# Layer 2 attention: a different table of steps for projections, value products and the copy of the inverses

## The reference

```python
def _L2_xattn_ref(x, context, mask, Wq, Wkv, Wout, b_out):
    HEADS = 16
    DIM_HEAD = 64
    SCALE = DIM_HEAD ** (-0.5)
    q = x @ Wq.T
    kv = context @ Wkv.T
    k, v = jnp.split(kv, 2, axis=-1)
    ...
    sim = jnp.einsum('bhid,bhjd->bhij', q, k) * SCALE
    sim = jnp.where(mask[:, None, None, :], sim, max_neg)
    attn = jax.nn.softmax(sim, axis=-1)
    out = jnp.einsum('bhij,bhjd->bhid', attn, v)
    out = out.transpose(0, 2, 1, 3).reshape(B, Nq, HEADS * DIM_HEAD)
    return out @ Wout.T + b_out
...
x = x + _L2_xattn_ref(_layernorm(x, axis=-1), ctx_1024, mask_BxS2_bf1, L2_xattn_Wq, L2_xattn_Wkv, L2_xattn_Wout, L2_xattn_b_out)
```

## Time and profile before

| | us |
|---|---|
| median of 3 executions | 1757.13 (1757.09 to 1757.54) |
| profiled execution | 1760.41 |
| its span | 1758.5 |
| mean granted clock | 0.926 |
| batch 0 from 494.56 | 51.27 |
| batch 1 from 545.83 | 61.81 |
| batch 2 from 607.64 | 65.05 |
| batch 3 from 672.69 | 63.47 |
| batch 4 from 736.16 | 61.81 |
| batch 5 from 797.97 | 61.81 |
| batch 6 from 859.78 | 61.82 |
| batch 7 from 921.60 to the end of its last inverse products, 981.80 | 60.20 |

### The profile page before, as it was taken

How to read it: one execution, slowest core, us unless ns; L and a number is a source line. 1 busy time by engine, 2 the same in 40 slices (tenths; PEclk the granted TensorE clock), 3 DMA queues, 4 the chain that set the end, 5 groups by cost and what they waited for, 6 DMA issues and landing times. The chain is left out here.

```text
span 1758.5 us, 44254 instructions
## 1 busy us (share of the span) xinstructions
PE 1535.7 (87%) x16764; PEld 804.3 (46%) x16764; DVE 1303.6 (74%) x3513; ACT 1032.9 (59%) x2227; POOL 569.5 (32%) x618
## 2 busy tenths in 40 slices
PE   5886999997669999999999899979799896999976
PEld 3532344433424444444554556655466652333333
DVE  5636778885878777677777789956899666799847
ACT  2331666665846555556555389854689631777764
POOL 0306656521010000000000289915799303342210
PEclk9895999998869999999999899999999985899997
DMA  5124333301010000000000000010100002322100
GB/s 167 34 31 134 76 80 67 66 14 49 1 38 3 8 2 9 8 3 9 28 3 3 8 1 1 0 40 9 48 1 0 1 14 74 55 43 50 30 2 24
DMA packets 60284, 54.21 MB, mean 31 GB/s; under 512 B 9610, under 2 KB 52798, under 8 KB 59974
## 3 DMA queue, kind: packets, MB, share of 16 engines
q1 hardware_dynamic: 59238, 51.32, 12.1%
q10 hardware_dynamic: 864, 0.39, 0.1%
HBM read 30.59 MB, written 1.05 MB: 18 GB/s over the span
## 5 line engine op out<-in xcount | busy, mean ns | idle before, releaser
L1926 ACT ACTIVATE probs_l2x<-probs_l2x,nmax_l2x 128x512 f32<-128x512 f32 x256 | 182.8, 715 | 193.5 <-DVE nmax_l2x L1797 193.5
L1797 DVE CUSTOM_DVE_ANT_0 probs_l2x<-s_ps_l2x,mask_b_l2x 128x512 f32<-128x512 f32 x256 | 166.6, 689 | 120.5 <-PE s_ps_l2x L2007 120.1
L1072 DVE CUSTOM_DVE_ANT_0 junk_l1x<-s_ps_l1x,mask_b_l1x 128x512 f32<-128x512 f32 x256 | 166.3, 687 | 50.3 <-PE s_ps_l1x L1273 46.0
L1075 DVE TENSOR_REDUCE nmax_l3x<-s_ps_l3x 128x1 f32<-128x512 f32 x256 | 163.7, 683 | 33.6 <-PE s_ps_l3x L1273 31.9
L1134 ACT ACTIVATE pT_l1x<-st_ps_l1x 128x1024 f32<-128x1024 f32 x128 | 131.2, 1025 | 79.9 <-PE st_ps_l1x L1258 79.5
L1809 DVE STREAM_TRANSPOSE pT_l2x<-probs_l2x 128x512 f32<-128x512 f32 x256 | 166.4, 688 | 0.0
L2007 PE MATMUL s_ps_l2x<-kT_l2x_first,q_l2x 64*32 64x512 f32 x2048 | 147.5, 634 | 11.3 <-DVE nmax_l2x L1797 10.5
L2023 PE MATMUL pv_ps_l2x<-pT_l2x,v_l2x_first 32*64 32x256 f32 x4096 | 137.7, 385 | 2.6 <-issue 2.6
L1740 POOL TENSOR_TENSOR spread_l2x<-inv_l2x,consts 128x512 f32<-128x512 f32 x16 | 17.6, 1101 | 324.5 <-DVE inv_l2x L1816 324.5
L2618 POOL TENSOR_TENSOR rn_l2a_first<-ssc_l2a_first,consts 128x16 f32<-128x16 f32 x28 | 109.1, 3897 | 20.2 <-DVE ssc_l2a_first L2645 20.0
L2788 ACT ACTIVATE probs_l2a<-minus_s_l2a,nmax_l2a 128x128 f32<-128x128 f32 (+1 forms) x256 | 106.1, 424 | 9.5 <-DVE nmax_l2a L2693 9.5
(11 more groups left out here) (531 smaller groups left out, 3574.9 us busy)
## 6 DMA issues: line engine op xcount, KB each, us to landing
mask_i_l1x<-in_mask SPq DMA_DIRECT2D x8, 512.0 KB, 4.2
maskT_i_l1x<-in_mask_t SPq DMA_DIRECT2D x8, 512.0 KB, 4.9
kT_l1x_first<-parts_l1x_first SPq DMA_DIRECT2D x60, 64.0 KB
kT_l3x_first<-parts_l3x_first SPq DMA_DIRECT2D x60, 64.0 KB
q_l1x<-parts_l1x_first SPq DMA_DIRECT2D x90, 32.0 KB
q_l3x<-parts_l3x_first SPq DMA_DIRECT2D x90, 32.0 KB
ctxT_l0x<-in_ctxT SPq DMA_DIRECT2D x9, 256.0 KB, 3.1
rows_l0x<-in_ctx SPq DMA_DIRECT2D x9, 256.0 KB, 4.2
```

The lines of the kernel that those rows point to most:

```text
L1072: dve.tensor_tensor_reduce(out=junk[w][:], in0=s_ps[w][:], in1=mask_b[b % 2][:, j, :], scale=-1.0, scalar=3e38, op0=ALU.add, op1=ALU.min, ...
L1075: dve.tensor_reduce(to, s_ps[w][:], AX.X, ALU.max, negate=True).then_inc(m.s_drained[w].sem, 1)
L1797: dve.tensor_tensor_reduce(out=probs[n % 4][:], in0=s_ps[w][:], in1=mask_b[b % 2][:], scale=-1.0, scalar=3e38, op0=ALU.add, op1=ALU.min, a ...
L1926: act.activation(probs[n % 4][:], probs[n % 4][:], ACT.Exp, bias=nmax[:, b % 2, n:n + 1], scale=-1.0, accum_out=sums[:, r, w, qb:qb + 1]). ...
```

## The change

The tables of steps are other ones. Value products stand in steps 3, 5 and 7 of a round, five, five and six blocks, where they stood in steps 1 to 7. Keys, queries and values are projected two to a step, mostly in steps without value products. V 6 and V 7 of a batch move to step 0 of the next batch (`after_batch`), the turning of the next batch's rows moves from step 7 to step 6, behind V 0 and V 1, and the output projection from steps 10 and 12 to 13 and 14, with the moments from step 13 to 14. In batch 7 the values V 2 to V 7 are projected in steps 8 to 10. On ScalarE the copy of the inverses comes behind the step's drains instead of ahead of them.

```diff
--- before.py
+++ after.py
@@ -1640,19 +1640,21 @@
 
     XT, Q, K, V, OUT, LOCAL = range(6)
     NQ, NV = NG // 2, 2 * CPB
-    this_batch = {0: [(K, 4), (K, 5), (K, 6)], 1: [(K, 7)], 2: [(Q, 2)], 3: [(Q, 3)], 4: [(V, 0)], 5: [(V, 1)], 6: [(V, 2)], 7: [(V, 3)],
-                  14: [(V, 4), (V, 5)], 15: [(V, 6), (V, 7)]}
-    next_batch = {7: [(XT, 0)], 8: [(K, 0), (K, 1), (K, 2)], 9: [(K, 3)], 11: [(Q, 0)], 13: [(Q, 1)]}
-    last_batch = {10: [(OUT, 0)], 12: [(OUT, 1)]}
-    end_values = {8: [(V, 4), (V, 5)], 9: [(V, 6), (V, 7)]}
+    this_batch = {1: [(K, 4), (K, 5)], 2: [(K, 6), (K, 7)], 4: [(Q, 2), (Q, 3)], 6: [(V, 0), (V, 1)], 8: [(V, 2), (V, 3)],
+                  14: [(V, 4)], 15: [(V, 5)]}
+    after_batch = {0: [(V, 6), (V, 7)]}
+    next_batch = {6: [(XT, 0)], 9: [(K, 0), (K, 1)], 10: [(K, 2), (K, 3)], 12: [(Q, 0), (Q, 1)]}
+    last_batch = {13: [(OUT, 0)], 14: [(OUT, 1)]}
+    end_values = {8: [(V, 2), (V, 3)], 9: [(V, 4), (V, 5)], 10: [(V, 6), (V, 7)]}
     for_local = {10: [0], 11: [1], 12: [2], 13: [3], 14: [4], 15: [5]}
-    blocks_of = {1: range(0, 3), 2: range(3, 6), 3: range(6, 8), 4: range(8, 10), 5: range(10, 12), 6: range(12, 14), 7: range(14, 16)}
+    blocks_of = {3: range(0, 5), 5: range(5, 10), 7: range(10, 16)}
 
     def step_jobs(b, s):
         end = b + 1 == B
         jobs = [(f, b - 1, n) for f, n in last_batch.get(s, ()) if b > 0]
         own = end_values if end and s >= QB else this_batch
         jobs += [(f, b, n) for f, n in own.get(s, ()) if b > 0 or f == Q]
+        jobs = [(f, b - 1, n) for f, n in after_batch.get(s, ()) if b > 1] + jobs
         jobs += [(f, b + 1, n) for f, n in next_batch.get(s, ()) if not end]
         if end:
             jobs += [(LOCAL, b, n) for n in for_local.get(s, ())]
@@ -1867,7 +1869,7 @@
                             invert_sums(n - 1)
                         for job in steps[b, s]:
                             drain(job)
-                        if s == 13 and b > 0:
+                        if s == 14 and b > 0:
                             out_moments(b - 1)
                         if s == 15 and b > 0:
                             out_scale(b - 1)
@@ -1943,10 +1945,10 @@
                         n = ROUNDS * b + s // QB
                         if ahead(b, s)[0] < B:
                             exponentials(*ahead(b, s))
+                        for job in steps[b, s]:
+                            drain(job)
                         if s % QB == 0 and n >= 2:
                             copy_inv(n - 2)
-                        for job in steps[b, s]:
-                            drain(job)
                 copy_inv(LAST - 1)
                 for job in behind[0:TPB]:
                     drain(job)
```

## The result

The changed kernel takes 1770.88 us (median of 6, 1764.98 to 1772.73) against 1757.11 (6, 1756.22 to 1757.54): ratio 1.0075, 95% interval 1.006 to 1.0091. It is slower by 13.8 us; forecast was 8. The profiled execution took 1770.07, its span 1768.2.

The account below looks back on a forecast made before the run. TensorE's own work plus its waits was taken to bound the stage. Without the clock the batches sum to +2.8 us, the clock adds +5.5, total +8.3: forecast 1765 us against 1757.13, range 1756 to 1774.

Parts of the forecast that it names:

- Part 1: TensorE's work in every batch: fewer groups of value products and paired projections save 2.64 us a batch.
- Part 2: First step of a round: the third key projection leaves, and its bank wait of 1.82 us goes, twice a batch.
- Part 3: Round's start: copy behind drains delays multiply and maxima; step 3's scores wait 2.07 us, K 6 0.39, together 2.46.
- Part 4: Step 6: turning the next batch's rows, third job behind two values, waits for a bank, +1.02 us a batch.
- The steady batch: Batches 2 to 6: each takes 61.47 us against 61.81, −0.34, together −1.7, slow clock steps apart.
- Batch 0: First batch of the stage: moved projections and low-clock steps make it 53.1 us against 51.3, +1.8.
- Batch 7: Last batch: +4.0 us; first round 28.0 against 28.9, second 34.6 against 29.7, through more values and late local tables.
- The clock: TensorE at round starts: idle stretches bring 8 half-clock steps at 1.5 us, less 6.45 before, +5.5 us.
- clock as before: Rival at round starts: same chain of waits but four slow steps as before, 1760 us; chance 0.20.
- every round: Rival at round starts: a slow step in all 14 rounds, +18.8, 1776 us; chance 0.10 for every round or nearly.
- the chain is hidden: Rival at round starts: the multiply does not hold step 2's maxima, batch 56.55 us, kernel 1726; chance 0.05.
- Half of it: Rival at round starts: drains delay the copy under 0.96 us or maxima start without the full gap, 1756; chance 0.13.

## Why the prediction was right, point by point

The forecast was 1765, slower with 0.68; measured is 1770.9, within the range. The sum had +8.3 and measured is +13.8: the clock was taken 5.2 too small and the rest of the stage 1.3, and 1.0 of that does not show in the medians. The spans of time between events came out to a few hundredths of a microsecond, the clock did not; the forecast held because its range was wide enough for that.

- **Part 1 (fewer groups, −2.64 a batch)**: right. The old and new tables with the copy in the same place differ by 2.5, waits taken off, and the profile after has value groups of 80, 80 and 96 instructions.
- **Part 2 (K 6's wait goes)**: right, in all 13 rounds.
- **Part 3 (the copy's chain)**: right in each event: copy, multiply, maxima, scores at T+4.24, 5.30, 6.60, 7.90, then K 6's wait of 0.33. A round without a slow step paid 2.47 us (11.23 less 8.76); batch 1's first, as worked out, 1.5. The experiments with the copy in two other places shift the scores to T+6.93 and T+6.14.
- **Part 4 (X)**: 1.04 of idle, 1.08 in the step (4.35 for 3.27 of work), worked out as 1.02. X one step later got 1.02 a batch back.
- **The steady batch**: 61.64 without slow steps, worked out as 61.47. Against 61.81 that is −0.17, not −0.34.
- **Batch 0**: +2.0, worked out as +1.8. **Batch 7**: +4.1 (steps 0 to 13 in 54.5 us in the kernel with the filled wait, the rest in 8.2, less the 58.6 of before without its slow step), worked out as +4.0.
- Without the clock this makes 2.0 − 1.15 − 0.85 + 4.1 = **+4.1**, where the sum had +2.8.
- **The clock**: this is the term that was mis-sized. I took 8 slow steps at 1.5 us; the profile has 11, at 4.65 to 5.04 us instead of 3.33, together 17.15. Less the 6.45 of before this is +10.7, not +5.5. Not among the 11 is a slow stretch of 1.7 us in the stage's last value products (from 997.96); before has one of 1.4 in its last output products instead. The bounds, 4 and 14, held the number; the choice between them was a guess from the one row of batch 0. Batches 4, 5 and 6 take 64.82, 64.83 and 64.84, and each round of them is hit. I read this as a state that repeats, in which the slow steps fix the length of a batch and the length brings the next slow steps; no experiment tests that. The row of batch 0 was also a poor guide: batch 1's first round idles 1.41, 1.42 and 0.33 us about groups of S and keeps the full clock in three profiles.
- **Profile and median**: I took the profiled execution's 3.3 us above the median to hold for both kernels. It does not: after's is 0.8 below its median. So the profiled executions differ by 9.7 and the medians by 13.8, and outside the stage the profiled executions differ by 5.3 the other way: that the stage's 14.8 comes so near the medians is partly luck. The profiled execution of before has four slow steps in its rounds, and its median is lower than it; how many its other executions had isn't known.

Of the rivals, "clock as before" is out (11 against 4), "every round" came near, and "the chain is hidden" is refuted by the 13 waits of 1.93 to 2.00 us. "Half of it" priced the copy first at a wait of 1.2 us a round; it was 1.5, since I had left out K 6's bank there.

The Trainium skill's page "TensorE: Matmul & The Clock Gate", section "A second HAM failure mode: psum-queue depth-cycling", has short idle stretches between groups make the clock swing between its levels. The 11 slow steps agree, and so does their going to one when the wait is filled. By it alone, every round would pay: three of the 14 did not, and with the copy first or ahead none did, where the idle stretches are 0.93 us or less from batch 1's second round on.

## What to carry to other kernels

When a wait is taken away, follow the in-order list of each engine to the next step and ask what was hidden behind it: here the maxima of the step after the next stood behind a multiply that stood behind a copy, and two drains put ahead of that copy cost 0.97 us a round. Work that an engine can do while it stands idle (the copy, ahead of the exponentials) belongs there, and a new table of steps should be tried with that order too before it is judged; these tables win 1.9 us a batch with the copy ahead (59.99 to 58.12) and lose 3.0 with it behind (61.80 to 64.83), all of it slow steps, since without them the batch is 61.64. Put a price on the clock as well as on the wait: here the exchanged copy cost 12.6 us in waits and 17.2 in slow steps.

## What the runs showed of the hardware

- Work of no use made the kernel faster: 28 more products of 512 columns (two for each of two K in 7 batches), nearly all ahead of a wait of 2.0 us, took the time from 1770.9 to 1756.6 us; in the profiled execution the granted clock stayed at 2.4 GHz in 13 of the 14 rounds, where it had fallen in 11.
- In one profiled execution each: of the 13 rounds that idle 1.93 to 2.00 and up to 0.33 us, the clock went to 1.2 GHz in 11; with the same waits and X one step later, in 6. With 0.84 to 0.93 and 0.33, 0.18 to 0.24 and 0.33, 0.91 and 0.83, or 0.91 us alone it fell in none, and with 1.82 alone in 4 of 13.
- The round that idles 1.41, 1.42 and 0.33 us, 3.2 in all, kept the full clock in three profiles, while one stretch of 1.82 was followed by the low clock in 4 of 13 rounds: the sum by itself doesn't tell whether the clock falls. Nor does the longest stretch: it fell after two of 1.40 in batch 0, and not after 1.93 and 0.33 in two rounds of the changed kernel.
